# Second attention's preparation: GpSimd adds the rotated values of the next token tile ahead of the low halves of the present one

## The reference, cut to what matters

```python
def _L1_attn_ref(x, W_qkv, W_o):
    def _apply_rope(x, theta=ROPE_THETA):
        ...
        xr = x.reshape(x.shape[:-1] + (d_k // 2, 2))
        rot = jnp.stack((-xr[..., 1], xr[..., 0]), axis=-1).reshape(x.shape)
        return x * jnp.cos(ang) + rot * jnp.sin(ang)
    ...
    qkv = jnp.einsum('bld,ed->ble', x, W_qkv)
    q, k, v = jnp.split(qkv, 3, axis=-1)
    ...
    q = _apply_rope(q)
    k = _apply_rope(k)
    att = jnp.einsum('bhqd,bhkd->bhqk', q, k) * scale
    att = jnp.where(causal, att, -jnp.inf)
    y = jnp.einsum('bhqk,bhkd->bhqd', softmax(att), v)
    return jnp.einsum('bld,ed->ble', y, W_o)
```

## Time and profile before

| what | value |
|---|---|
| three timed runs | 821.83, 829.54, 829.76 us (median 829.54) |
| profiled execution, its own time | 822.29 us |
| its span, first to last instruction | 820.5 us |
| PE busy | 710.4 us (87%) |
| DVE busy | 617.7 us (75%) |
| ACT busy | 456.3 us (56%) |
| POOL busy | 398.4 us (49%) |
| mean granted TensorE clock | 0.938 of full speed |

### The profile page before, as it was taken

How to read it: one execution, slowest core, us unless ns; L and a number is a source line. 1 busy time by engine, 2 the same in 40 slices (tenths; PEclk the granted TensorE clock), 3 DMA queues, 4 the chain that set the end, 5 groups by cost and what they waited for, 6 DMA issues and landing times. The chain is left out here.

```text
span 820.5 us, 17560 instructions
## 1 busy us (share of the span) xinstructions
PE 710.4 (87%) x5515; PEld 479.9 (58%) x5515; DVE 617.7 (75%) x1436; ACT 456.3 (56%) x1033; POOL 398.4 (49%) x412
## 2 busy tenths in 40 slices
PE   7899869999979999999898699854797598979984
PEld 3555447777646777655455466433695487645652
DVE  5878877778687777699977677544998597676656
ACT  3545668888758888646423266315574475324551
POOL 5554866666656666358536277324005320341340
PEclk8999989999989999999999899967899598998998
DMA  9999996000000000030001243300000010013324
GB/s 370 331 295 210 209 255 2 0 0 0 2 0 1 0 0 0 1 123 1 1 14 59 79 123 106 129 1 0 2 2 1 14 40 2 1 53 88 115 85 166
DMA packets 64945, 59.07 MB, mean 72 GB/s; under 512 B 29106, under 2 KB 59186, under 8 KB 64370
## 3 DMA queue, kind: packets, MB, share of 16 engines
q1 hardware_dynamic: 60706, 47.85, 23.7%
q0 software_dynamic: 3744, 10.26, 3.5%
q10 hardware_dynamic: 432, 0.15, 0.1%
HBM read 27.92 MB, written 30.33 MB: 71 GB/s over the span
## 5 line engine op out<-in xcount | busy, mean ns | idle before, releaser
L1511 PE MATMUL PS<-XT,WA 128*128 128x512 f16 x432 | 100.1, 379 | 0.0
L616 POOL TENSOR_TENSOR ARENA<-ARENA,ST 128x512 f32<-128x512 f32 x64 | 66.6, 1040 | 64.0 <-DVE ST L1291 64.0
L734 ACT ACTIVATE ARENA<-PS 128x512 f16<-128x512 f32 (+1 forms) x48 | 28.5, 593 | 85.9 <-DVE PS L1169 79.7
L1511 PE MATMUL PS<-WA,ARENA 128*128 128x256 f16 (+2 forms) x960 | 68.2, 212 | 6.1 <-DVE ARENA L1178 5.0
L575 POOL DMA_INDIRECT yt_rows<-WA,DIX x46 | 45.1, 979 | 54.8 <-ACT WA L866 40.6
L1511 PEld LDWEIGHTS PS<-WA,ARENA 128*128 128x128 f16 x960 | 56.5, 97 | 21.9 <-DVE ARENA L1178 11.0
L1511 PEld LDWEIGHTS PS<-XT,WA 128*128 128x128 f16 (+1 forms) x432 | 42.2, 98 | 44.0 <-issue 0.8
L1511 PE MATMUL PS<-KVR,ARENA 128*128 (+1 forms) x384 | 58.9, 282 | 7.6 <-DVE ARENA L1263 5.1
L1511 PE MATMUL PS<-XT,WC 128*128 128x512 f16 x264 | 62.2, 386 | 2.4 <-DVE T L1160 1.4
L1271 DVE TENSOR_REDUCE ST<-PS 128x2 f32<-128x512 f32 x64 | 44.0, 687 | 26.0 <-PE PS L1511 25.1
L767 ACT ACTIVATE ARENA<-PS,ST 128x256 f32<-128x256 f32 x128 | 59.4, 471 | 7.0 <-DVE ST L1274 6.8
(11 more groups left out here) (186 smaller groups left out, 1790.3 us busy)
## 6 DMA issues: line engine op xcount, KB each, us to landing
xs_rows<-ROUT SPq DMA_DIRECT2D x2, 9252.0 KB, 46.1
WA<-xs_rows SPq DMA_DIRECT2D x46, 129.0 KB
WB<-wb_dram SPq DMA_DIRECT2D x1, 4096.0 KB, 21.5
WC<-wc_dram SPq DMA_DIRECT2D x1, 2304.0 KB, 27.5
WA<-wa_dram SPq DMA_DIRECT2D x4, 512.0 KB, 7.1
WA<-wa_dram SPq DMA_DIRECT2D x1, 2048.0 KB, 12.8
WA<-yt_rows SPq DMA_DIRECT2D x4, 512.0 KB, 4.1
WB<-yt_rows SPq DMA_DIRECT2D x4, 512.0 KB, 5.8
```

Source lines behind the costliest of these rows:

```text
L616: pl.tensor_tensor(pr, pr, rs.broadcast_to([P, 2, S]), ALU.mult).then_inc(norm_done, 1)
L734: sc.activation(HH[r, a, 0, :], hidden_tile(f, hf, j, a), ACT.Copy).then_inc(hid_hi, 1)
L1511: ins = te.matmul(dst, left(a), right(b), start=first and n == 0, stop=last and n == 2, skip_group_check=True)
```

## The change

In GpSimd's program the add of tile i + 1 is issued ahead of the low halves of tile i, within each half. The add of a half's first tile stands ahead of the loop. In the second half, `turn(6, 0)` stood behind the low halves of that half's tile 1; it now stands behind the add of its tile 2 and ahead of the low halves of its tile 1. The programs of the other engines and all semaphore counts are as before.

```diff
             turn(4, 0)
+            rotated1(0, 0)
             for i in range(TPH):
-                rotated1(i, i % 2)
+                if i + 1 < TPH:
+                    rotated1(i + 1, 1 - i % 2)
                 qk1_low(i, i % 2)
             turn(4, 1)
+            rotated1(TPH, 0)
             for i in range(TPH):
-                rotated1(TPH + i, i % 2)
-                qk1_low(TPH + i, i % 2)
+                if i + 1 < TPH:
+                    rotated1(TPH + i + 1, 1 - i % 2)
                 if i == 1:
                     turn(6, 0)
+                qk1_low(TPH + i, i % 2)
             scatter(6, 0)
```

## The result

The changed kernel takes 842.06 us (median of 4 runs, 840.46 to 844.54); the kernel before 825.75 us (median of 4, the three runs above and one more; 821.83 to 829.76). The ratio is 1.0185, 95% interval 1.0146 to 1.0224: slower by 15 us, or by 12 to 18; the two medians lie 16.3 us apart. The profiled execution took 841.34 us with a span of 839.5, against 822.29 and 820.5.

A forecast was written before the change was run, and what follows sets the result against it. No engine was full; the stage was taken as a chain of waits. Added losses of 7.9 us in the first half and 8.8 in the second, +16.7, gave 839.0 or 846.2 us by footing; forecast 842, range 832 to 851.

The forecast's parts named there:

- The queue: GpSimd's queue is strictly first in, first out, so a tile's low halves wait behind the next tile's add, input ready.
- The first half, +7.9: Second attention's preparation, first half: 5.0 us from the serialized order plus 2.1 and 0.8 of slow TensorE clock.
- The loop at full clock: Low halves, transposes, products, rotation and next add in series: 7.43 us from one tile's low halves' end to the next.
- the clock: TensorE's longer waits bring half clock in its bursts: 2.1 + 0.8 us in the first half, 2.1 in the second.
- one of T0 and T1 as slow: First half: of the first two tiles' transposes, one counted at half clock, 2.1 us with the products behind it.
- My choice by the length of the wait: TensorE bursts after waits clearly over 3.69 us run at half clock; after 2.8 us they do not.
- The second half, +8.8: Second attention's preparation, second half: 6.7 us from the serialized order, normalization ahead of low halves included, plus 2.1 of clock.
- 0.8 less, for L1089: Second half: a router-rank instruction of 1.26 us beside the last tile's low half gets shorter, giving back 0.8 us.
- a gain that I had called possible and not counted: Transposes already slow before could regain full clock: 0.8 us each, 2.4 in all; none counted.
- The sum: Profiled 822.3 us plus 16.7 from both halves gives 839.0.
- The footing: Two of three timed runs lay 7.2 us above the profiled one; on theirs 846.2, so 842 was chosen between.

The follow-up runs named there:

- L1's place in the order: Against the kernel before, only each half's second-tile add issued ahead of the first tile's low halves, later adds as before: 828.47 us, ratio 1.0018.
- the loop's length: New order in the first half alone, TensorE's products and VectorE's rotations of tiles 2 and 3 moved earlier: 825.68 us, 0.9997 to the kernel before.
- Idle products: Products of zeros and ones filling TensorE's waits: added to the full change 839.02 us, to the kernel before 825.47; ratios to before 1.0153 and 0.9985.
- the best version: Kernel before with adds of rotated values moved from GpSimd to VectorE and TensorE kept busy with products of zeros and ones: 817.55 us, ratio 0.9893.
- the version with the adds alone: Kernel before with only the adds of rotated values moved from GpSimd to VectorE, both halves: 821.39 us, ratio 0.9953.

## Why the prediction was right, step by step

**The queue.** Right, and shown: L1 stood behind R2 with its input ready 7.5 us before it ran (554.37 to 561.84). Both remedies, L1's place in the order and the loop's length, took most of the first half's loss of 9.8 us away: 2.0 and 0.3 us were left.

**The first half, +7.9.** It was 9.8. The loop at full clock was right to 0.02 us (7.45 measured). Two terms were small. L0 came 1.8 us later relative to R0, not 1.2, since R1 had to wait 1.82 us for rotation 1, which ended 3.01 us after R0's start instead of 2.40. The change does not reach the products that this rotation waits for; the granted clock was 0.50 and 0.69 in the two microseconds from 548 here, and 0.77 and 1.00 in the two from 547 before. And the clock took 4.1, not 2.9: products behind T0 1.2 (rotation 3.70 after T0, not 2.47), T1 with its products 2.1 (4.53, not 2.47), T2 0.8. I had counted only one of T0 and T1 as slow; T0 itself was fast, and its products were not. My choice by the length of the wait (slow when clearly over 3.69 us) did not hold: T0 was fast after 4.36, T3 slow after 2.16, T7 slow after 1.53.

**The second half, +8.8.** It was 7.4. L4 ended 7.05 us after R4, against 4.83 (+2.2, as predicted); L5 16.64 against 9.60 (+7.0, predicted 6.9, normalization included); T6 25.64 against 16.60 (+9.0, predicted 7.5 and 2.1 of clock; the clock took 1.3, rotation 7 coming 3.78 us after T5 instead of 2.47).

From T6 to the scores it then took 7.41 us instead of 9.06. I had 0.8 less, for L1089, and the reason was wrong: the router's ranks are not on this path. Before, T7 (641.62) waited for L7, not for ScalarE's copies of tile 6, which ended at 640.81:

```profile
639.79 1.02 ACT L844 ACTIVATE KVR<-PS 64x1024 f16<-64x1024 f16 x1
640.04 1.43 POOL L646 TENSOR_TENSOR ARENA<-T,ARENA 128x512 f16<-128x512 f32 x1
```

In the new order L7 ends at 660.19, the copies at 661.41, and T7 (661.47) waits for the copies. T7 starts 3.37 us after T6 instead of 5.03; from T7 to the scores it is 4.0 us in both. Of the 1.65 us, 0.66 is T6 itself, 1.21 instead of 1.87 us, a gain that I had called possible and not counted. The other 1.0 is that ScalarE starts its copies sooner and T7 no longer waits for L7. L1089 did get shorter (L1093 after, 0.42), but in the old order it could reach the path only through L646, which took 1.43 us beside it instead of 1.15. So the 0.8 was near by luck.

**The sum.** 822.3 + 16.7 = 839.0 against 841.3 for the profiled execution. Of the 2.3 us missing, 0.5 is in the stages (17.2 against 16.7). The rest lies outside them, and 0.9 ahead of the stage and -0.9 behind it cancel: from the first scores to rotation 4 the profile of before had 47.43 us, and every other kernel here 48.0 to 49.4, those with an untouched first half included. So that 1.7 us looks like a short execution before rather than the change; with one profile of the kernel before it is argued, not shown. The 16.7 itself came out near 17.2 because the halves were off to opposite sides, by 1.9 too little and 1.4 too much.

**The footing.** I moved the forecast up by 3 us because two of three runs lay at 829.5 to 829.8. With more runs the median of before is 825.64 to 826.83, about half-way, and 825.75 + 16.7 is 842.45. That the forecast of 842 met 842.06 is luck in its closeness: the footing was a guess between two values, and the errors of the halves cancelled.

## What to carry to other kernels

Before issuing a producer ahead of a consumer on an in-order engine, follow what the producer itself waits for: if its chain leads through the consumer being delayed, as here R2 through T0 to L0, the reorder makes a loop out of a pipeline. With two buffers, tile i + 2 always depends on tile i, so running one tile ahead is free only if enough work is left beside that dependency: here 3.88 us from L0 to the rotated tile 2 had R1, its wait and L1 beside them before, and nothing after. Moving the small step to an engine that has its inputs at hand, here the add onto VectorE, gave the overlap that the reorder could not.

## What the runs showed of the hardware that was not expected

Idle products do keep TensorE's clock up, but they are in its queue: at full clock 12 of them took 2.75 us, at half clock 4.78, and what stood behind them waited. One long wait behind them undid their effect (3.28 us for VectorE in the old order, 3.60 us ahead of T5 in the new).

VectorE's add of two SBUF tiles was slowed beside GpSimd's low halves; its rotation, which reads PSUM, was not (0.69 us beside a low half at 550.80 in the best version). The add in that version, beside no GpSimd work 0.69 us, beside a low half 1.69:

```profile
549.11 0.69 DVE L1353 TENSOR_TENSOR T<-T 128x512 f32<-128x512 f32 x1
...
552.19 1.69 DVE L1353 TENSOR_TENSOR T<-T 128x512 f32<-128x512 f32 x1
```

It goes the other way too, though not each time: a low half beside such an add took 1.60 us instead of 1.15 in the version with the adds alone, but 1.15 beside the add of 1.69 us above. The Trainium skill (GPSIMD Engine Reference, key structural facts) has the two engines share their SBUF ports; these rows agree. In them an add moved to VectorE was cheapest where GpSimd was idle.
